# Slot-list matmuls as a TensorE loop over experts, with bf16 dummy matmuls in loops

## The reference

```python
S = jax.nn.sigmoid(xt @ Wg).T                 # 8 x 2048
G, I = jax.lax.top_k(S, k)                    # k = 512
ex = xt[I]
hid = gelu(jnp.einsum('ekh,ehf->ekf', ex, W1) + b1[:, None, :])
out = (jnp.einsum('ekf,efh->ekh', hid, W2) + b2[:, None, :]) * G[..., None]
new_x = jnp.zeros_like(xt).at[I.reshape(-1)].add(out.reshape(-1, h))
```

## Time and profile before

| | us |
|---|---|
| median of three runs | 420.55 |
| the profiled execution | 423.39 |
| its span, first to last instruction | 421.6 |

### The profile page before, as it was taken

The page is one execution under the profiler, slowest core; times in us unless marked ns, Lnnn a source line. Parts: engine busy times, 40 slices in busy tenths (PEclk is TensorE's granted clock), DMA queues, the critical chain, the costliest instruction groups (busy, mean ns, idle before and its releaser), DMA issues.

```text
span 421.6 us, 7457 instructions
## 1 busy us (share of the span) xinstructions
PE 319.4 (76%) x2394; PEld 153.1 (36%) x2394; DVE 271.8 (64%) x549; ACT 204.0 (48%) x392; POOL 180.5 (43%) x207
## 2 busy tenths in 40 slices
PE   8898797999999999999989982111739897680930
PEld 6543342333333333333334441001424665450630
DVE  4789876989999999999968746777611332220210
ACT  1665314888888888888876521000303233220200
POOL 4376515567411111111113703000544877788662
PEclk9999855999999999999999996555767999986885
DMA  8436731111111111111006004300032556544321
GB/s 237 126 117 206 256 107 34 38 40 40 40 40 40 40 39 39 39 39 39 3 3 176 2 7 118 108 0 0 19 85 78 121 121 144 112 93 66 32 26 18
DMA packets 34489, 30.40 MB, mean 72 GB/s; under 512 B 5280, under 2 KB 28704, under 8 KB 34464
## 3 DMA queue, kind: packets, MB, share of 16 engines
q1 hardware_dynamic: 28320, 23.65, 18.1%
q0 software_dynamic: 6144, 6.43, 9.2%
HBM read 18.27 MB, written 11.60 MB: 71 GB/s over the span
## 4 chain that ended last, share of the span: by engine, by line
PE 42%; DVE 21%; POOL 16%; issue 12%; ACT 4%; DMA 3%; ACTq 0%; DVEq 0%; SPq 0%; POOLq 0%
PE ps L1311 14%; POOL out L560 11%; PE ps L1274 9%; PE ps L1297 6%; DVE mx L868 4%; POOL ex L549 4%; DVE big L1021 3%; DMA out<-big,idx 2%; PE ps L1324 2%; ACT osb L679 2%; PE ps L1539 1%; DVE KB L904 1%; PE ps L1550 1%; PE ps L1169 1%; DVE big L1120 1%
## 5 line engine op out<-in xcount | busy, mean ns | idle before, releaser
L868 DVE TENSOR_REDUCE mx<-ps 128x2 f32<-128x1024 f32 x128 | 148.7, 1219 | 12.2 <-PE ps L1274 12.2
L702 ACT ACTIVATE big<-ps 128x512 f32<-128x512 f32 x256 | 139.3, 598 | 27.4 <-PE ps L1297 25.4
L1311 PE MATMUL ps<-big,VA 128*32 128x256 f32 (+1 forms) x960 | 80.1, 405 | 3.0 <-ACT osb L679 2.5
L549 POOL DMA_INDIRECT ex<-rows,idx x32 | 34.1, 1064 | 57.9 <-DVE idx L1125 40.7
L1274 PE MATMUL ps<-KB,QB 48*128 48x512 bf16 x256 | 52.6, 411 | 6.4 <-DVE mx L868 4.2
L1297 PE MATMUL ps<-QB,KB 51*128 51x512 bf16 x256 | 55.2, 385 | 1.8 <-ACT osb L679 1.1
L560 POOL DMA_INDIRECT out<-big,idx x32 | 50.6, 1580 | 13.1 <-issue 9.1
L755 ACT ACTIVATE big<-ps,b1c 128x512 f32<-128x512 f32 x32 | 22.0, 687 | 65.0 <-PE ps L1539 60.2
L1539 PE MATMUL ps<-big,w1s 128*128 128x512 f32 x64 | 36.1, 685 | 3.7 <-DVE big L1091 3.3
L429 POOL TENSOR_TENSOR VA<-Vall,bv_row 128x128 f32 (+1 forms) x16 | 7.2, 453 | 72.3 <-PE ps L1311 72.3
L1311 PEld LDWEIGHTS ps<-big,VA 128*32 128x32 f32 x960 | 19.3, 107 | 36.5 <-issue 34.8
(11 more groups left out here) (194 smaller groups left out, 424.6 us busy)
## 6 DMA issues: line engine op xcount, KB each, us to landing
KB<-k_parts SPq DMA_DIRECT2D x32, 96.0 KB
QB<-q_parts SPq DMA_DIRECT2D x32, 96.0 KB
w1s<-in_w SPq DMA_DIRECT2D x8, 256.0 KB
w2s<-in_w SPq DMA_DIRECT2D x8, 256.0 KB
k_parts<-big SPq DMA_DIRECT2D x4, 384.0 KB, 3.2
q_parts<-big SPq DMA_DIRECT2D x4, 384.0 KB, 4.7
QB<-mxp SPq DMA_DIRECT2D x96, 2.0 KB
rows<-rw SPq DMA_DIRECT2D x1, 1088.0 KB, 6.0
```

The source lines that it names most:

```text
L549: pool.indirect_dma_start(out=ex[:, e % 2, c, :], out_offset=None, in_=rows_dram, in_offset=bass.IndirectOffsetOnAxis(ap=idx[:, e, c:c + 1 ...
L702: nc.scalar.activation(PT[:, u, 2 * i + half, kc, :], ps[:, EXP_BANKS[n], :], ACT.Exp, scale=SCALE).then_inc(s_ex, 1)
L868: nc.vector.tensor_reduce(mx[:, u, :].rearrange("p (h a) -> p h a", h=2)[:, :, n], ps[:, max_bank(u, n):max_bank(u, n) + 2, :], AX.X, ALU.max,
L1311: ins = mm(ps[32 * j:32 * j + 32, 6, cols], VA[:, u, kc, j, :], PT[:, u, j, kc, cols], start=kc == 0 and not cols.start, stop=kc == TC - 1 ...
```

## The change

On TensorE the sixteen matmuls of one expert become the body of a hardware loop over the chunk's experts, with operands whose addresses depend on the loop's register. Each round raises a new semaphore `s_list` once, and ScalarE waits for as many rounds as there are experts done. `s_slot` loses this increment, so its counts go from three to two for each chunk. `keep_warm` goes; ahead of each chunk stands a loop of four bf16 dummies of `stay_warm` on bank 5, with 4 rounds (16 dummies) ahead of chunk 0, where there were none, and 9 rounds (36 dummies) ahead of chunk 1.

```diff
+        s_list = sem("s_list")
@@ ScalarE
-                act.wait_ge(s_slot, 3 * n + 1)
+                act.wait_ge(s_list, last)
                 cols = slice(first * 32, last * 32)
                 nc.scalar.activation(slots[0:16, cols], ps[0:16, SLOT_BANK[n], cols], ACT.Copy).then_inc(s_slot, 1)
@@ VectorE
-                dve.wait_ge(s_slot, 3 * n + 3)
+                dve.wait_ge(s_slot, 2 * n + 2)
@@ TensorE
-            def keep_warm(n):
-
-
-                for _ in range(n):
-                    mm(ps[:, 4, :], ident[:], wmod[:, 0:512], start=True, stop=True)
@@
             for n, (first, last) in enumerate(CHUNKS):
-                if n == 1:
-                    keep_warm(4)
+                with pe.Fori(0, (4, 9)[n]):
+                    stay_warm(4, 5)
                 pe.wait_ge(s_one_ab, n + 1)
                 if n == 1:
                     pe.wait_ge(s_one_t, 1)
-                for e in range(first, last):
+                with pe.Fori(first, last) as e:
                     for s in range(NSEG):
-                        ins = mm(ps[0:16, SLOT_BANK[n], 32 * e:32 * e + 32], one_a[:, e * NSEG + s, :],
-                                 one_b[:, e * NSEG + s, :], start=s == 0, stop=s == NSEG - 1)
-                ins.then_inc(s_slot, 1)
-                pe.wait_ge(s_slot, 3 * n + 2)
+                        at = [v[:, ds(e * NSEG + s, 1), :].rearrange("p o a -> p (o a)") for v in (one_a, one_b)]
+                        ins = mm(ps[0:16, SLOT_BANK[n], ds(e * 32, 32)], at[0], at[1],
+                                 start=s == 0, stop=s == NSEG - 1)
+                    ins.then_inc(s_list, 1)
+                pe.wait_ge(s_slot, 2 * n + 1)
```

## The result

| | us |
|---|---|
| before, median of four runs | 419.52 (417.47 to 420.82) |
| after, median of four runs | 453.25 (452.20 to 453.86) |
| ratio, 95% interval | 1.0797 (1.0761 to 1.0833) |
| the profiled execution of after, its span | 453.61, 451.8 |

The changed kernel is 33.7 us slower. The forecast was 433.1 us, 12.6 us slower, with a range of 424 to 446: the sign is right, the size is wrong by 20 us and the range does not hold the time.

What follows compares the result with a forecast made beforehand. The prediction took a GpSimd queue of gathers and scatters, delayed by TensorE's slot matmuls through VectorE's indices, as the bound. Chunk 0 +4.9 us and chunk 1 +7.7 us gave +12.6 us: 420.55 to 433.1 us, range 424 to 446.

Steps and rivals of the forecast that it cites:

- the number of register groups: TensorE slot loop: one fused register group per matmul, 0.15 us a matmul, eight rounds costing +12.6 us in sum.
- I am low by up to 11 us: TensorE slot loop: the forecast's stated error if the register groups are split in two.
- the upper bound: TensorE slot loop: a fused group plus one plain register instruction per matmul, 4.3 us a round, +24 us.
- the 7 us of gaps: Slot matmuls of chunk 1 on TensorE: about 7 us lost to slow dispatch, which the loop would remove.
- Nothing of the loop is dispatched before VectorE's release: Start of each chunk's slot loop on TensorE: rounds start after VectorE's wait, 0.1 us from wait to first matmul.
- The dummies cost nothing: Dummy loops ahead of both chunks: hidden in VectorE's cover, 0, and up to 0.5 us in the worst case.
- sparse slot matmuls give no reason for more: Stage before the up projection: the granted clock is 0.50 and sparse matmuls give no reason for a higher one.
- The tail moved as one piece: GpSimd queue from expert 3's gathers at 325.25 on: whatever moves that start moves the end by the same amount.
- (a): Rival, slot loop: loop costs little and gaps go, below about 60 ns a matmul; 416.7 us, down to 414; chance 0.14.
- (b): Rival, slot loop: a round at its low bound or a little above, loss near 6.5 us, 427; no separate chance.
- (c): Rival, slot loop: register-addressed weight loads and matmuls each cost like register instructions; +38 us, 458.6; chance 0.04.
- (d): Rival, slot matmuls: gaps stay, loop cost is small, and the two cancel within 2 us; chance 0.05.

Runs made afterwards that it cites:

- cheap_addr: The changed kernel with operand offsets each a multiple of the loop register plus a constant, so matmuls need no product of their own: 440.45 us, ratio 1.0337.
- before_c: The kernel before, unchanged, run and traced again in the last batch: 419.13 us, ratio 0.9999.
- before_a: The kernel before, unchanged, run as a kernel of its own for its trace: 419.04 us.
- dummies_only: The kernel before with only the new bf16 dummy loops for the four fp32 dummies, slot matmuls straight-line: 425.65 us, ratio 1.0004.
- micro: The kernel before plus five loops of 4 x 16 idle slot-sized matmuls with differing address arithmetic ahead of the counting rounds: 454.07 us, including added work.
- wide_warm: The wide kernel plus 20 bf16 dummies ahead of the first turn: 418.84 us, ratio 0.9968 to the kernel before.
- wide: The kernel before with all experts of a chunk in one matmul per segment, no loop: 421.32 us, ratio 0.9890; repeated, 420.59 us, 0.9993.
- dummies_only_2: The dummies_only kernel, unchanged, run again in the last batch: 419.39 us, ratio 0.9984.

## Why the prediction was wrong

**The failed step** is the number of register groups: the sum took each matmul "with a fused group of about 0.085 us", one, and the forecast looked for "a fused register group for each". No run of the changed kernel shows one for each; after has two (256 for 128 matmuls). That one would do was my estimate. I priced one well (0.15 us forecast, 0.16 measured in cheap_addr), and named the case of two, "I am low by up to 11 us"; it is 0.262 us a matmul and a round of 4.79 us, where I had 2.9 and, as the upper bound, 4.3. The bound was built by adding a plain instruction of 0.095 us; a second fused group adds 0.10, and the round's own cost is 0.56 to 0.60 us, where the forecast had 0.5 and its upper bound only 0.4. Eight rounds with their releases take 9.6 us (298.56 to 308.12) and 29.1 us (314.96, VectorE's end, to 344.05), 38.7 us where I had 23.4 in all: 15.3 us of the miss.

**The second failed step** is the baseline. I credited the change with "the 7 us of gaps". The four runs of before that the median comes from were not traced, but at 417.47 to 420.82 us they stand where the runs beside dense traces stand: chunk 1 takes 2.6 us there and not 9.8. That is 7 us of the miss, of which 1.9 us come back, since in a dense execution the first turn waits for expert 0's rows until 1.9 us later than in after, where it waits for nothing (L1523 directly behind L1551). 15.3 + 7 - 1.9 = 20.4 us, and the forecast was 20.2 us too low. The sum with the right terms, against before_c: chunk 0 9.6 - 1.1 = +8.5, chunk 1 29.1 - 2.6 = +26.5, less 1.9 = +33.1 us. The stage measures 50.6 - 17.5 = +33.1, the medians +33.7 and, in the last batch, +31.0.

The sign of this error could have been seen. The profiled execution stood 3 us above the runs, and I noted the difference and made the sum against it, as if the 3 us were the profiler's. A profile by itself does not cost that: the profiled execution of before_a took 419.26 us, beside 25 other runs of the same kernel in its batch between 418.49 and 421.88.

**What held.** Nothing of the loop is dispatched before VectorE's release, as forecast (the MOVEs start at 298.6 and 315.0, the releases are at 298.56 and 314.96), though the way from release to first matmul is 0.5 to 0.6 us and not 0.1. The dummies cost nothing: 16 take 3.14 us and 36 take 6.71 us (forecast 2.9 to 3.4 and 6.4). The forecast's 0.18 us for one was read "with the clock mostly at half"; the trace gives a granted clock of 1.00 for that stretch, 1.4 to 5.4 us of before, so the agreement says nothing on the clock. The 36 end 0.3 us after VectorE's release at 314.96, yet the first slot matmul comes at 315.46, 0.5 us behind the release, no later than in chunk 0, where they end 1 us before it; dummies_only confirms it twice. Most of the first up projection (346.63 to 352.75) runs at a clock of 0.50 (6.12 us at a mean of 0.60, before 6.32 at 0.58): the forecast that sparse slot matmuls give no reason for more is right. Windows of after, granted clock behind the five engines:

```profile
330.00:340.00 10.00, 6.25 (x33) 2.89 (x33) 0.00 (x0) 0.00 (x0) 0.00 (x0) 0.50 0.00 0
...
348.00:350.00 2.00, 2.00 (x3) 0.67 (x2) 0.00 (x0) 0.69 (x1) 1.70 (x2) 0.50 0.20 49
350.00:352.00 2.00, 2.00 (x4) 0.86 (x3) 0.00 (x0) 0.77 (x2) 1.39 (x3) 0.62 0.29 87
```

From 330 to 340 TensorE is the only engine at work. The tail moved as one piece, as forecast: 107.07 against 107.09 us. Expert 3's gathers start at 355.26 rather than 338, by the same error.

**The rivals.** (a) is out: it needed 60 ns a matmul. (b), the low bound, is out. (c) comes near the measured time, 458.6 against 453.25, by the wrong mechanism: it had one group and a price on weight load and matmul themselves, and micro's 27 ns with addresses in registers refute that; a time alone would have seemed to confirm it. (d) is out. Of (a), "a small loop needs no fetch" is not refuted: in after no block of instructions is fetched from 299 to 308 nor from 318 to 344, and one is between 317 and 318, in the first round of chunk 1. It wins nothing: with no fetch beside it, a round measures 4.79 us, of which the branch lasts 0.21 us (COMPARE_BRANCH, median 208 ns).

**A version beside both.** wide_warm keeps the full clock for the first up projection, 1.00 from 309 to 317.5, where wide fell to 0.50 by 311 (TensorE's timeline):

```profile
309.71 2.36 PE L1171 MATMUL ps<-ones 128*128 128x256 bf16 x20
312.37 0.66 PE L1530 MATMUL ps<-ident,ex 128*128 128x128 f32 x4 [0.30 <-DMA ex<-rows,idx]
313.81 3.70 PE L1541 MATMUL ps<-big,w1s 128*128 128x512 f32 x8 [0.78 <-DVE big L1092]
```

3.70 us where before_a needs 5.59 at a mean clock of 0.66 and the shown trace 6.32 at 0.58. Yet it gains only 0.3% on before (interval 0.1 to 0.5%): the gathers of expert 3 then follow GpSimd's own queue. What the 20 dummies give over wide alone isn't measured, since wide didn't run in that batch. wide alone gains nothing in the dense batch (0.9993) and 1.1% in the gapped one. The slot matmuls cost 1.02 + 2.56 = 3.6 us in the dense stage, beside a GpSimd queue that is full; there was never much to win on TensorE here, and much to lose.

## What to carry to other kernels

Count the register groups before pricing a loop. Here each group of arithmetic on addresses cost the sequencer some 0.07 to 0.085 us on top of its own duration (0.131 - 0.046 and 0.158 - 0.074 us in micro, half of 0.262 - (0.051 + 0.074) us in after), and small matmuls stayed near 30 ns in a loop only with constants (29 ns) or addresses held in registers (41 ns with the stop between rounds), against 0.13 to 0.16 us with one group and 0.26 us with two. Read the rows of the weight loads too: in micro's second loop, matmul rows that last 0.19 us each hide a stop of about 0.2 us between them. The stall of "issue" in the shown trace was a loss of that execution, 423.39 us beside runs of 417.47 to 420.82; compare the profiled time with the timed runs, and profile the same kernel again, before a gain is booked on such a stall. When a time agrees with a rival's, look at the rows that the rival names before believing it.

## What the runs showed of the hardware

- A loop's branch cost nothing in a loop with constant addresses: four rounds of sixteen went through in 1.88 us without a gap (micro, L1514). With addresses held in registers the loads of a round are as dense, 0.49 us, and stop for 0.17 to 0.21 us between rounds (L1517). With arithmetic for each matmul TensorE idles 0.42 to 0.67 us between rounds (micro 0.42 at L1521 and 0.43 to 0.53 at L1525, cheap_addr 0.56 to 0.67, after 0.56 to 0.60).
- The straight-line 29 ns matmuls were held up in some executions, five matmuls every 0.75 or 1.44 us, 9.8 us for 96 in place of 2.56 (before against before_a), and not at all in others, with the same program and one block of instructions fetched beside it in both; the batch that had it was 5 to 6 us slower (425.67 against 420.06 to 420.65). What decides was not found.
- Thirty-six dummies of 256 columns took 4.11 us at a granted clock of 1.00 (dummies_only_2, 298.36 to 302.47) and 6.71 us in after, where it stood at 0.50 from within the slot matmuls of chunk 0 (0.54 from 300 to 304) until about 314, most of the dummies' time. At the start of before, 22 took 3.93 us with the trace's clock at 1.00: 0.18 us each against 0.11.
